# Expert feed-forward: the first two token tiles of an expert as a pair with the weights stationary

## Chip, cores and metric

One core of a Trainium2 chip runs the whole program. The time is device microseconds (us) of one execution; the kernel before has a median of 1525.64 us over three runs (1524.73 to 1525.66).

## What is computed

A transformer layer on 2 x 1024 tokens of width 512. After a layer norm, the output is the sum of the input, causal attention (16 heads, 4 key groups), a shared two-layer network, and a mixture of 32 experts of which each token uses 6. Cut to the part that the change touches:

```python
idx, w = _route(xf, Wr, br)                    # 6 experts for each of 2048 tokens
gate = zeros((T, E)).at[arange(T)[:, None], idx].add(w)
def step(acc, ew):
    w1, w2, g = ew                             # w1 256 x 512, w2 512 x 256
    h = square(relu(xf @ w1.T)) @ w2.T
    return acc + g[:, None] * h, None
```

Only the chosen tokens are computed. The six choices of 2048 tokens are 12288 rows, which the router sorts by expert into tiles of 128 rows, each expert's last one filled up.

## The kernel before, in words

There are three stages. The first normalises and routes the tokens and computes the shared network. The second, which the change rebuilds, runs the experts. The third runs the attention of eight groups and adds the experts' rows, fetched by index.

Every product of 32-bit values is made of three matmuls on reduced-width values: an upper half (`_hi`) and a lower half (`_lo`, what the upper half leaves out), as upper x upper, upper x lower and lower x upper. ScalarE makes each upper half by a copy, VectorE each lower half by a subtraction.

The program of the expert stage is written out by hand, one in-order list for each engine, and every hand-over is a semaphore count. `over_experts` loops over 8 rounds of 4 experts; inside, a body per expert takes its tiles `lo` to `hi`, which `count_tiles` has worked out from the routing (at least 2 tiles each). A tile's steps are:

- GpSimd gathers 128 token rows into one of four slots of `xg`.
- TensorE turns them (`transpose_gathered`, four 128-column matmuls into `ps_x`), a tile ahead of their use; ScalarE copies the upper half (`upper_tokens`), VectorE the lower (`lower_tokens`).
- `hidden_tile`: 12 matmuls of 256 columns, tokens stationary, first-layer weights moving.
- ScalarE takes relu (`relu_hidden`), VectorE squares (`square_hidden`), TensorE turns the squares (`transpose_hidden`, two 128-column matmuls), ScalarE and VectorE make halves again (`upper_hidden`, `lower_hidden`).
- `output_tile`: 6 matmuls of 512 columns; ScalarE copies the result to `ysb` (`copy_output`), SyncE stores it to memory.

TensorE's list is one tile deep: first layer of tile p and the turn of tile p+1's tokens, second layer of tile p-1, turn of tile p's squares. So the second layer of an expert's last tile stands inside the next expert's body.

The weights of an expert are 1 MB of raw values. SyncE loads them into one of two buffers `eraw`, three experts ahead; ScalarE and VectorE convert them in four pieces (`upper_weights`, `lower_weights`) into one of four slots, two experts ahead. SyncE's list is in order too, and is what `store_tiles` says:

```python
sp.wait_ge(ew_lo, (e + (NSH + 2)) * WP)
sp.dma_start(eraw[:, (s + AHEAD) % 2, :], we[bass.ds((e + AHEAD) * P, P), :])
...
with sp.Fori(lo, hi) as p:
    ...
    sp.wait_ge(y_copied, past(p + 1))
    sp.dma_start(y_d[bass.ds(p * P, P), :], ysb[:, ...])
```

The load for expert e+3 thus stands behind the store of the last tile of expert e-1, which waits for that tile's output copy. The change leaves SyncE's and GpSimd's lists as they are.

In the first stage the router marks, for every token tile, which of at most `MAXT` = 160 tiles its rows go to (`mark_rows` on VectorE, rows `tile_hot` of `MAXT` columns), and the memory of the tiles that might stay unused is filled with zeros by one DMA from ScalarE's queue.

Of the kernel before, what the change touches and what calls it, by code (L numbers as in the profile page):

```python
# [6 lines left out]
F32 = mybir.dt.float32  # L7
# [38 lines left out]
MAXT = MINT + 2 * E  # L46
XG = 4
YB = 4
# [80 lines left out]
def moe_attention_kernel(nc, x, wa, we, wr, br, out):  # L129
# [11 lines left out]
    with ExitStack() as ctx:  # L141
# [75 lines left out]
        with ExitStack() as room:  # L217

            xg = sb("xg", [P, XG, D], F32, room)
            xgT_hi = sb("xgT_hi", [P, KD, P], F32R, room)  # L220
            xgT_lo = sb("xgT_lo", [P, KD, P], F32R, room)
# [3 lines left out]
            hT_hi = sb("hT_hi", [P, KM, P], F32R, room)  # L225
            hT_lo = sb("hT_lo", [P, KM, P], F32R, room)
# [38 lines left out]
        ps_y = ps_s[:, 3, :]  # L265

# [391 lines left out]
        def _(pe):  # L658
# [190 lines left out]
            def transpose_gathered(slot, q):  # L849
                pe.wait_ge(xg_in[slot], (q // XG + 1) * 16)  # L850
                for k in range(KD):
                    mm = pe.transpose(ps_x[:, k * P:(k + 1) * P], xg[:, slot, k * P:(k + 1) * P], ident[:, :])
                mm.then_inc(mx_ready, 1)

            def hidden_tile(p, s):
# [3 lines left out]
                for k in range(KD):  # L859
                    pe.matmul(ps_h, xgT_hi[:, k, :], w_hi[:, k, :], start=(k == 0), stop=False)  # L860
                    pe.matmul(ps_h, xgT_hi[:, k, :], w_lo[:, k, :], start=False, stop=False)  # L861
                pe.wait_ge(mx_lo, p + 1)
                for k in range(KD):
                    mm = pe.matmul(ps_h, xgT_lo[:, k, :], w_hi[:, k, :], start=False, stop=(k == KD - 1))  # L864
                mm.then_inc(mh_ready, 1)
                q = p + 1
                with pe.If(q // 2 % 2 == 0):
                    with pe.If(q % 2 == 0):
                        transpose_gathered(0, q)
                    with pe.Else():  # L870
                        transpose_gathered(1, q)
                with pe.Else():
                    with pe.If(q % 2 == 0):
                        transpose_gathered(2, q)
                    with pe.Else():
                        transpose_gathered(3, q)

            def output_tile(p, s):

                w_hi, w_lo = w2(hi_slot(s)), w2(lo_slot(s))  # L880
                pe.wait_ge(mhhi_ready, past(p + 1))
                for m in range(KM):
                    pe.matmul(ps_y, hT_hi[:, m, :], w_hi[:, m, :], start=(m == 0), stop=False)  # L883
                    pe.matmul(ps_y, hT_hi[:, m, :], w_lo[:, m, :], start=False, stop=False)  # L884
                pe.wait_ge(mhlo_ready, past(p + 1))
                for m in range(KM):
                    mm = pe.matmul(ps_y, hT_lo[:, m, :], w_hi[:, m, :], start=False, stop=(m == KM - 1))  # L887
                mm.then_inc(my_ready, 1)

            def transpose_hidden(p, weights=None):  # L890
                pe.wait_ge(mhsq_ready, past(p + 1))
                for m in range(KM):
                    if m and weights is not None:

                        pe.wait_ge(ew_lo, weights)
# [9 lines left out]
            def expert_tiles(e, s, lo, hi, es):  # L905

                pe.wait_ge(ew_lo, (e + NSH) * WP + 2)
                hidden_tile(lo, slot_of(s))
                after = pair_bound(pe, e + 2)
                if s:  # L910
                    output_tile(lo - 1, slot_of(s - 1))
                else:
                    with pe.If(es > 0):
                        output_tile(lo - 1, slot_of(SLOTS - 1))
# [9 lines left out]
            output_tile(last - 1, slot_of(SLOTS - 1))  # L924
# [95 lines left out]
        def _(act):  # L1020
# [206 lines left out]
            def upper_tokens(q):  # L1227

                act.wait_ge(mx_ready, q + (1 + XG))
                act.activation(xgT_hi[:, :, :], ps_x.rearrange("p (k n) -> p k n", k=KD), ACT.Copy).then_inc(mx_hi, 1)  # L1230
# [12 lines left out]
            def upper_hidden(p):  # L1243
# [570 lines left out]
```

## Time and profile before

| what | value |
|---|---|
| median of three runs | 1525.64 us |
| profiled execution | 1526.73 us, span 1525.0 us |
| TensorE busy | 1509.9 us (99% of the span) |
| VectorE / ScalarE / GpSimd busy | 1132.8 / 837.9 / 298.3 us |
| moved by DMA | 184.34 MB, mean 121 GB/s |
| chain that ended last | 96% TensorE, 2% VectorE, 1% DMA |
| granted TensorE clock | 0.999 of full |

The span is the profiled execution from its first to its last instruction; 1.7 us lie around it. An engine's busy time says how full it is, not whether it decides. "Idle before" and its releaser say what an instruction waited for. A time that has a row of its own is a start, in us from the start of the span. Two instructions that start 0.12 us apart and last 0.28 us overlap in the engine's pipeline: the distance of the starts is what one costs in a row.

### The profile page before, as it was taken

The page shows a single profiled execution, that of the slowest core. Times are in us where ns is not written, and L with a number is a line of the kernel's source. Part 1 is how long each engine was busy: PE and PEld are TensorE (multiplying, and loading weights), DVE is VectorE, ACT ScalarE, POOL GpSimd, SP SyncE. Part 2 cuts the span into 40 slices and gives each one's busy share as a digit, 9 for nine tenths or more (in the row PEclk, how much of TensorE's full clock was granted, in tenths as well). Part 3 has the DMA queues.
Part 4 walks back from the last instruction along what each step waited for, and adds up shares of the span by engine and source line. Part 5 has one row for each costly group of instructions (what it writes and reads, how often), then busy time and mean ns, then how long its engine had stood idle before and what let it go on. Part 6 is the DMA issues. An engine that isn't in the chain of part 4 may idle for free.

```text
span 1525.0 us, 31150 instructions
## 1 busy us (share of the span) xinstructions
PE 1509.9 (99%) x8552; PEld 1302.1 (85%) x8553; DVE 1132.8 (74%) x2586; ACT 837.9 (55%) x1753; POOL 298.3 (20%) x540
## 2 busy tenths in 40 slices
PE   9998999999999999999999999999999999999998
PEld 8877998899899888888888888888888888888886
DVE  7896666666666669859949948967975994994896
ACT  5574666666666635535625635644553553553553
POOL 0003344334344311011002002102102101200211
PEclk9999999999999999999999999999999999999999
DMA  8874777777876612102102103422211210210111
GB/s 318 301 302 165 218 243 233 229 234 228 258 234 207 228 35 70 43 21 76 55 7 79 45 28 120 149 62 85 67 34 41 69 41 21 76 34 28 56 42 55
DMA packets 64774, 184.34 MB, mean 121 GB/s; under 512 B 7136, under 2 KB 7264, under 8 KB 60000
## 3 DMA queue, kind: packets, MB, share of 16 engines
q1 hardware_dynamic: 39888, 112.56, 21.1%
q0 software_dynamic: 16640, 54.54, 13.1%
q10 hardware_dynamic: 8208, 16.78, 2.8%
q8 instruction: 19, 0.31, 0.1%
q14 instruction: 19, 0.16, 0.0%
HBM read 123.29 MB, written 60.56 MB: 121 GB/s over the span
## 4 chain that ended last, share of the span: by engine, by line
PE 96%; DVE 2%; DMA 1%; issue 0%; ACT 0%; ACTq 0%; DVEq 0%; SPq 0%
PE bank L663 8%; PE bank L665 8%; PE bank L993 8%; PE bank L664 8%; PE ps_s L663 7%; PE ps_s L665 7%; PE ps_s L664 7%; PE ps_s L980 5%; PE ps_s L982 5%; PE ps_s L981 4%; PE ps_s L860 4%; PE ps_s L883 4%; PE ps_s L864 3%; PE ps_s L861 3%; PE ps_s L887 3%; PE ps_s L884 3%
## 5 line engine op out<-in xcount | busy, mean ns | idle before, releaser
L1322 ACT ACTIVATE probs<-probs,negmax 128x128 f32<-128x128 f32 (+7 forms) x256 | 197.4, 774 | 122.5 <-DVE negmax L1736 121.9
L1330 ACT ACTIVATE pT_hi<-bank 128x512 fp32r<-128x512 f32 x288 | 164.5, 595 | 143.4 <-PE bank L993 117.5
L1347 DVE TENSOR_TENSOR pT_lo<-bank,pT_hi 128x512 fp32r<-128x512 f32 x288 | 189.7, 684 | 41.0 <-ACT pT_hi L1330 40.0
L1736 DVE CUSTOM_DVE_ANT_0 probs<-ps_s,causal 128x128 f32<-128x128 f32 (+7 forms) x256 | 189.5, 753 | 17.1 <-PE ps_s L982 14.9
L427 POOL TENSOR_TENSOR settled<-ident 128x1 f32<-128x1 f32 x192 | 46.5, 242 | 788.7 <-DVE acc L1765 778.7
L993 PE MATMUL bank<-ident,probs 128*128 128x128 f32 x1152 | 157.0, 272 | 0.0
L993 PEld LDWEIGHTS bank<-ident,probs 128*128 128x128 f32 x1152 | 136.9, 141 | 19.8
L663 PE MATMUL ps_s<-xT_hi,wa_hi 128*128 128x512 f32 x384 | 152.7, 398 | 0.0
L665 PE MATMUL ps_s<-xT_hi,wa_lo 128*128 128x512 f32 x384 | 150.9, 393 | 0.0
L664 PE MATMUL ps_s<-xT_lo,wa_hi 128*128 128x512 f32 x384 | 150.2, 391 | 0.0
L1745 DVE TENSOR_SCALAR probs<-probs,rnorm 128x128 f32<-128x128 f32 (+7 forms) x256 | 133.4, 521 | 9.1
L980 PE MATMUL ps_s<-kT_hi,qT_hi 128*128 128x512 f32 (+5 forms) x384 | 134.0, 349 | 1.0 <-DVE qT_lo L1716 0.5
L982 PE MATMUL ps_s<-kT_hi,qT_lo 128*128 128x512 f32 (+5 forms) x384 | 131.2, 342 | 0.0
L981 PE MATMUL ps_s<-kT_lo,qT_hi 128*128 128x512 f32 (+5 forms) x384 | 130.9, 341 | 0.0
L663 PE MATMUL bank<-pT_hi,v_hi 128*128 128x512 f32 x288 | 123.6, 429 | 0.6 <-DVE cT_lo L1347 0.6
L623 POOL DMA_INDIRECT xg<-normed_tokens,comb_idx x112 | 111.8, 998 | 23.3 <-issue 18.1
L1347 DVE TENSOR_TENSOR hT_lo<-ps_s,hT_hi 128x256 fp32r<-128x256 f32 x111 | 47.2, 425 | 92.0 <-ACT hT_hi L1245 53.5
L665 PE MATMUL bank<-pT_hi,v_lo 128*128 128x512 f32 x288 | 113.5, 394 | 0.0
L1251 ACT ACTIVATE ysb<-ps_s 128x512 f32 x111 | 66.5, 599 | 84.9 <-PE ps_s L887 65.7
L664 PE MATMUL bank<-pT_lo,v_hi 128*128 128x512 f32 x288 | 112.7, 391 | 0.0
L652 POOL DMA_INDIRECT comb<-expert_outputs,comb_idx x96 | 105.2, 1096 | 19.6 <-issue 11.5
L663 PE MATMUL bank<-wa_hi,cT_hi 128*128 128x512 f32 x256 | 101.5, 396 | 1.4 <-DVE cT_lo L1347 1.4
(197 smaller groups left out, 3596.3 us busy)
## 6 DMA issues: line engine op xcount, KB each, us to landing
eraw<-we SPq DMA_DIRECT2D x37, 1024.0 KB
expert_outputs<-ysb SPq DMA_DIRECT2D x111, 256.0 KB
araw<-wa SPq DMA_DIRECT2D x37, 512.0 KB, 4.3
expert_outputs<-comb ACTq DMA_DIRECT2D x1, 16384.0 KB, 47.4
normed_tokens<-xn SPq DMA_DIRECT2D x4, 1024.0 KB, 10.0
out<-acc SPq DMA_DIRECT2D x16, 256.0 KB
acc<-x SPq DMA_DIRECT2D x2, 1024.0 KB, 13.8
turned_tokens<-xT_hi SPq DMA_DIRECT2D x2, 1024.0 KB, 7.6
```

Of the source, the lines that this page charges most:

```text
L663: pe.matmul(out_, lh, rh, start=(first and k == 0), stop=False)
L664: pe.matmul(out_, lh, rl, start=False, stop=False)
L665: mm = pe.matmul(out_, ll, rh, start=False, stop=(last and k == parts - 1))
L980: pe.matmul(o, q_h, kT_hi[:, ks], start=True, stop=False)
L981: pe.matmul(o, q_h, kT_lo[:, ks], start=False, stop=False)
L982: mm = pe.matmul(o, q_l, kT_hi[:, ks], start=False, stop=True)
L993: mm = pe.transpose(ps_t[blk % 2][:, h * P:(h + 1) * P], probs[:, i % 2, h, a * P:(a + 1) * P], ident[:, :])
L1322: act.activation(pr, pr, ACT.Exp, bias=negmax[:, i % 2, a:a + 1], scale=-1.0, accum_out=rowsum[:, i % 2, a:a + 1]).then_inc(exp_ready, 1)
L1330: act.activation(pT_hi[:, blk % RING, :], ps_t[blk % 2][:, :], ACT.Copy).then_inc(pt_hi_ready, 1)
L1347: dve.tensor_tensor(out_, whole, upper.bitcast(F32), ALU.subtract).then_inc(signal, 1)
L1736: dve.tensor_tensor_reduce(halves(probs[:, i % 2, a, 0:keys]), ps_s[:, s:s + parts, 0:keys // parts], halves(causal[:, SQ - keys:]), -1.0, ...
L1745: dve.tensor_scalar(pr, pr, rnorm[:, i % 2, a:a + 1], None, ALU.mult).then_inc(probs_ready, 1)
```

## The change

An expert has at least three tiles now (`LEAST`), and its first two are taken as a pair. `hidden_pair` runs the first layer with the weights stationary and the tokens of both tiles moving (256 columns), once for each half of the hidden units, so its result stands with hidden units on partitions and need not be turned. ScalarE takes its relu and its square, which is at once the upper half; VectorE squares and subtracts. The second tile's tokens are turned at the head of the body into a bank of their own (`ps_x2`). The second layer of the expert before's last tile is split: its upper half's matmuls stand ahead of the pair's first layer, its lower half's behind it and behind the third tile's turn. The second layer of the pair's first tile follows in the body (`output_first`), that of the second in the loop. In the loop, the turn of the squares stands between the upper and the lower half of the second layer. `hT_hi` and `hT_lo` have two sets and a place for either tile. The list of tiles grows from 160 to 177 columns, and so do the marks and the zero fill. The attention's first maximum on VectorE waits for the expert stage's stores, since its buffer shares memory with the new ones.

```diff
-MAXT = MINT + 2 * E
+LEAST = 3
+MAXT = max(LEAST * (E - n) + min(n * TILES, (T * TOPK + (P - 1) * n) // P) for n in range(E + 1))
...
+            def hidden_pair(lo, s):
...
+                both = lambda x, k: x[:, k, :, :].rearrange("p t n -> p (t n)")
+                for m in range(KM):
+                    ms = slice(m * P, (m + 1) * P)
+                    if m == 0:
+                        pe.wait_ge(mx_hi, lo + 2)
+                    for k in range(KD):
+                        pe.matmul(ps_p[m], w_hi[:, k, ms], both(xgT_hi, k), start=(k == 0), stop=False)
+                        pe.matmul(ps_p[m], w_lo[:, k, ms], both(xgT_hi, k), start=False, stop=False)
+                    if m == 0:
+                        pe.wait_ge(mx_lo, lo + 2)
+                    for k in range(KD):
+                        mm = pe.matmul(ps_p[m], w_hi[:, k, ms], both(xgT_lo, k), start=False, stop=(k == KD - 1))
+                    mm.then_inc(mh_ready, 1)
...
             def expert_tiles(e, s, lo, hi, es):
 
-                pe.wait_ge(ew_lo, (e + NSH) * WP + 2)
-                hidden_tile(lo, slot_of(s))
-                after = pair_bound(pe, e + 2)
+                turn_tokens(lo + 1, ps_x2)
                 if s:
-                    output_tile(lo - 1, slot_of(s - 1))
+                    output_upper(lo - 1, s - 1, ps_y2)
...
-                transpose_hidden(lo, (e + (NSH + 1)) * WP)
-                with pe.Fori(lo + 1, hi) as p:
+                after = pair_bound(pe, e + 2)
+                pe.wait_ge(ew_lo, (e + NSH) * WP + 2)
+                hidden_pair(lo, slot_of(s))
+                pe.sem_inc(mt_ready, 2)
+                turn_tokens(lo + 2, ps_x)
+                if s:
+                    output_lower(lo - 1, s - 1, ps_y2)
...
+                pe.wait_ge(ew_lo, (e + (NSH + 1)) * WP)
+                output_first(lo, s)
+                with pe.Fori(lo + 2, hi) as p:
                     hidden_tile(p, slot_of(s))
-                    output_tile(p - 1, slot_of(s))
+                    pe.wait_ge(y_copied, past(p - 1))
+                    output_upper(p - 1, s, ps_y)
                     transpose_hidden(p)
+                    output_lower(p - 1, s, ps_y)
                 return after
...
             def expert_uppers(e, s, lo, hi, es):
...
-                relu_hidden(lo)
-                upper_tokens(lo + 1)
-                upper_weights(0, slot, arrived)
                 if s:
-                    copy_output(lo - 1)
+                    upper_tokens(lo + 1, 1)
...
-                upper_hidden(lo)
+                upper_weights(0, slot, arrived)
                 after = pair_bound(act, e + 2)
                 upper_weights(1, slot, arrived)
-                with act.Fori(lo + 1, hi) as p:
+                relu_pair(lo, 0)
+                upper_pair(lo, 0, s)
+                upper_weights(2, slot, arrived)
+                relu_pair(lo, 1)
+                upper_pair(lo, 1, s)
+                upper_tokens(lo + 2)
+                if s:
+                    copy_output(lo - 1, ps_y2)
...
+                copy_output(lo, ps_y)
+                upper_weights(3, slot, arrived)
+                with act.Fori(lo + 2, hi) as p:
                     relu_hidden(p)
                     upper_tokens(p + 1)
-                    copy_output(p - 1)
-                    upper_hidden(p)
-                upper_weights(2, slot, arrived)
-                upper_weights(3, slot, arrived)
+                    upper_hidden(p, s)
+                    copy_output(p - 1, ps_y)
```

VectorE's list follows ScalarE's in the same order. How the lists of the built programs read, first ScalarE in the body of the second expert, before. `mrelu` is the relu, `xgT_hi` the turned tokens, `w_hi` a piece of weights (it needs the raw load), `ysb` the output copy, `hT_hi` the hidden upper half:

```order
L1241 ACTIVATE mrelu<-ps_s 128x256
L1229 REGISTER_ALU
L1230 ACTIVATE xgT_hi<-ps_s 128x512
L1234 ISA
L1235 ACTIVATE w_hi<-eraw 128x512
L1251 ISA
L1251 ACTIVATE ysb<-ps_s 128x512
```

The output copy is the fourth piece of work in the body. The same place of the changed kernel, from the head of the body (`prelu` is the pair's relu):

```order
L1280 ACTIVATE xgT_hi<-bank 128x4x128
...
L1286 ACTIVATE w_hi<-eraw 128x512
...
L1298 ACTIVATE prelu<-bank 128x256
...
L1303 ACTIVATE hT_hi<-prelu 128x256
L1286 ACTIVATE w_hi<-eraw 128x512
L1298 ACTIVATE prelu<-bank 128x256
...
L1303 ACTIVATE hT_hi<-prelu 128x256
...
L1280 ACTIVATE xgT_hi<-ps_s 128x4x128
L1314 ISA
L1314 ACTIVATE ysb<-bank 128x512
```

The output copy of the expert before (`ysb<-bank`) now stands behind both relus and squares of the pair, the third tile's tokens and three pieces of weights (the second of them is in a gap here), and the first piece stands ahead of the relus. TensorE's loop body, for the tiles that are not in the pair, before:

```order
L852 MATMUL ps_s<-ident,xg 128x128 x4
...
L883 MATMUL ps_s<-wa_hi,hT_hi 128x512
L884 MATMUL ps_s<-wa_lo,hT_hi 128x512
L883 MATMUL ps_s<-wa_hi,hT_hi 128x512
L884 MATMUL ps_s<-wa_lo,hT_hi 128x512
L887 MATMUL ps_s<-wa_hi,hT_lo 128x512 x2
L891 REGISTER_ALU
L896 MATMUL ps_s<-ident,mhsq 128x128 x2
```

and now:

```order
L858 MATMUL ps_s<-ident,xg 128x128 x4
...
L920 MATMUL ps_s<-wa_hi,hT_hi 128x512
L921 MATMUL ps_s<-wa_lo,hT_hi 128x512
L920 MATMUL ps_s<-wa_hi,hT_hi 128x512
L921 MATMUL ps_s<-wa_lo,hT_hi 128x512
L932 REGISTER_ALU
L934 MATMUL ps_s<-ident,mhsq 128x128 x2
L928 MATMUL ps_s<-wa_hi,hT_lo 128x512 x2
```

The turn of the squares has moved ahead of the last two matmuls of the second layer.

## Rows read from the trace of the kernel before

**Rows 1.** Busy time of each engine in two stretches, with header: expert stage, first gap.

```profile
core 0: us, PE busy (x) PEld busy (x) DVE busy (x) ACT busy (x) POOL busy (x), PEclk, DMA share, GB/s
138.00:140.00 2.00, 0.00 (x0) 0.00 (x0) 2.00 (x5) 0.45 (x1) 1.38 (x3) 1.00 0.69 254
135.80:534.10 398.30, 393.70 (x2665) 352.61 (x2664) 246.84 (x467) 265.19 (x572) 158.24 (x323) 1.00 0.73 233
```

**Rows 2.** Costliest groups of 140 to 540 us, by shape: turns of squares.

```profile
L896 PE MATMUL ps_s<-ident,mhsq 128*128 128x128 f32 x222 | 42.8, 274 | 2.6 <-DVE mhsq L1653 2.3 <-issue 0.3
```

**Rows 3.** Timeline of TensorE, one tile of the stage (start, duration, instruction).

```profile
163.05 0.38 PE L896 MATMUL ps_s<-ident,mhsq 128*128 128x128 f32 x2
...
163.39 0.28 PE L861 MATMUL ps_s<-wa_lo,xgT_hi 128*128 128x256 f32 x1
...
164.22 0.65 PE L864 MATMUL ps_s<-wa_hi,xgT_lo 128*128 128x256 f32 x4
164.70 0.60 PE L852 MATMUL ps_s<-ident,xg 128*128 128x128 f32 x4
165.06 0.47 PE L883 MATMUL ps_s<-wa_hi,hT_hi 128*128 128x512 f32 x1
165.37 0.39 PE L884 MATMUL ps_s<-wa_lo,hT_hi 128*128 128x512 f32 x1
...
166.06 0.62 PE L887 MATMUL ps_s<-wa_hi,hT_lo 128*128 128x512 f32 x2
166.52 0.38 PE L896 MATMUL ps_s<-ident,mhsq 128*128 128x128 f32 x2
```

**Rows 4.** Timeline of TensorE, ScalarE, VectorE: start of one expert, its output copy, conversions.

```profile
205.69 0.36 PE L860 MATMUL ps_s<-wa_hi,xgT_hi 128*128 128x256 f32 x1
...
209.38 0.60 ACT L1251 ACTIVATE ysb<-ps_s 128x512 f32 x1 [0.30 <-PE ps_s L887]
...
214.33 0.60 PE L852 MATMUL ps_s<-ident,xg 128*128 128x128 f32 x4
214.53 0.38 ACT L1241 ACTIVATE mrelu<-ps_s 128x256 f32<-128x256 f32 x1 [0.64 <-PE ps_s L864]
...
214.95 0.42 DVE L1653 TENSOR_TENSOR mhsq<-mrelu 128x256 f32<-128x256 f32 x1 [0.60 <-ACT mrelu L1241]
...
218.29 0.39 ACT L1241 ACTIVATE mrelu<-ps_s 128x256 f32<-128x256 f32 x1
...
218.56 0.61 ACT L1230 ACTIVATE xgT_hi<-ps_s 128x512 fp32r<-128x512 f32 x1
...
219.04 0.65 ACT L1235 ACTIVATE wa_hi<-eraw 128x512 fp32r<-128x512 f32 x1
```

**Rows 5.** Timeline of SyncE's queue: weight loads, output stores between them.

```profile
211.29 0.35 SPq L490 DMA_DIRECT2D eraw<-we  x1
214.04 7.27 SPq L500 DMA_DIRECT2D expert_outputs<-ysb  x3
221.77 0.35 SPq L490 DMA_DIRECT2D eraw<-we  x1
```

**Rows 6.** Timelines of SyncE's queue and ScalarE: weight loads and conversions that waited.

```profile
137.37 0.33 SPq L472 DMA_DIRECT2D eraw<-we  x1
...
142.19 0.63 ACT L1235 ACTIVATE w_hi<-eraw 128x512 fp32r<-128x512 f32 x1 [3.73 <-DMA eraw<-we]
...
247.33 0.35 SPq L490 DMA_DIRECT2D eraw<-we  x1
...
255.37 0.63 ACT L1235 ACTIVATE w_hi<-eraw 128x512 fp32r<-128x512 f32 x1 [0.78 <-DMA eraw<-we]
...
356.36 0.35 SPq L490 DMA_DIRECT2D eraw<-we  x1
...
364.65 0.63 ACT L1235 ACTIVATE wa_hi<-eraw 128x512 fp32r<-128x512 f32 x1 [0.22 <-DMA eraw<-we]
```

**Rows 7.** Busy time of each engine in two stretches after the load of 221.77.

```profile
222.50:228.00 5.50, 5.50 (x40) 4.97 (x39) 2.47 (x5) 2.92 (x7) 2.66 (x6) 1.00 0.90 355
228.00:228.50 0.50, 0.50 (x6) 0.50 (x6) 0.42 (x1) 0.00 (x0) 0.00 (x0) 1.00 0.08 33
```

**Rows 8.** DMA issues of the page, timelines of ScalarE's queue and VectorE: fill, marks.

```profile
expert_outputs<-comb ACTq DMA_DIRECT2D x1, 16384.0 KB, 47.4
...
55.37 0.44 ACTq L1183 DMA_DIRECT2D expert_outputs<-comb  x1
...
112.69 2.87 DVE L1526 TENSOR_SCALAR tile_hot<-lane,xf,tok_f 128x160 f16<-128x160 f16 x12
```

More of the change, by code:

```diff
@@ L265, in moe_attention_kernel @@
         ps_y = ps_s[:, 3, :]
+        ps_x2 = banks[0][:, :]
+        ps_p = [bank[:, 0:2 * P] for bank in banks[1::2]]
+        ps_y2 = banks[2][:, :]
         consts_in = sem("consts_in")
@@ new lines, in output_first @@
+            def output_first(lo, s):
+                w_hi, w_lo = w2(hi_slot(slot_of(s))), w2(lo_slot(slot_of(s)))
+                for m in range(KM):
+                    pe.wait_ge(mhhi_ready, past(lo + (m + 1)))
+                    pe.matmul(ps_y, hT_hi[:, s % 2, m, 0, :], w_hi[:, m, :], start=(m == 0), stop=False)
+                    pe.matmul(ps_y, hT_hi[:, s % 2, m, 0, :], w_lo[:, m, :], start=False, stop=False)
+                    pe.wait_ge(mhlo_ready, past(lo + (m + 1)))
+                    mm = pe.matmul(ps_y, hT_lo[:, s % 2, m, 0, :], w_hi[:, m, :], start=False, stop=(m == KM - 1))
+                mm.then_inc(my_ready, 1)
@@ L885, in output_tile, with output_lower, transpose_hidden @@
+            def output_lower(p, s, bank):
+                w_hi = w2(hi_slot(slot_of(s)))
                 pe.wait_ge(mhlo_ready, past(p + 1))
                 for m in range(KM):
-                    mm = pe.matmul(ps_y, hT_lo[:, m, :], w_hi[:, m, :], start=False, stop=(m == KM - 1))
+                    mm = pe.matmul(bank, hT_lo[:, s % 2, m, 1, :], w_hi[:, m, :], start=False, stop=(m == KM - 1))
                 mm.then_inc(my_ready, 1)
-            def transpose_hidden(p, weights=None):
+            def transpose_hidden(p):
@@ L1259, in _ @@
             upper_tokens(0)
+            upper_tokens(1, 1)
             for c in range(WP):
@@ L1682, in expert_lowers @@
                 slot = slot_of(s + 2)
[L1683 to L1684 removed]
+                if s:
+                    lower_tokens(lo + 1, 1)
+                else:
+                    with dve.If(es > 0):
+                        lower_tokens(lo + 1, 1)
                 lower_weights(e + 2, 0, slot)
[L1686 removed]
                 after = pair_bound(dve, e + 2)
                 lower_weights(e + 2, 1, slot)
[L1689 removed]
+                square_pair(lo, 0)
+                lower_pair(lo, 0, s)
+                lower_weights(e + 2, 2, slot)
+                square_pair(lo, 1)
+                lower_pair(lo, 1, s)
+                lower_tokens(lo + 2)
+                lower_weights(e + 2, 3, slot)
+                with dve.Fori(lo + 2, hi) as p:
                     square_hidden(p)
                     lower_tokens(p + 1)
[L1692 to L1694 removed]
+                    lower_hidden(p, s)
                 return after
```

121 lines of the change are left out of this document (73 added, 48 removed).

## Prediction

> **What bounds the kernel now.** I read the busy times of the stage first, then TensorE's timeline, then the queue that feeds the weights. In the expert stage (135.80 to 534.10 us) TensorE is busy 393.70 of 398.30 us, while ScalarE and VectorE have a third of the stage free and the DMA engines work at 0.73 of their time [rows 1]. So TensorE sets the end, and whatever leaves its list comes back as time, as long as nothing else becomes late. The stage has 111 tiles: 222 turns of squares, two a tile [rows 2]. One undisturbed tile lasts 163.05 to 166.52, 3.47 us [rows 3]. It is 12 first-layer matmuls of 256 columns at 0.119 us (seven steps from 163.39 to 164.22), 6 second-layer matmuls of 512 columns at 0.23 us (three steps from 165.37 to 166.06), and six 128-column turns, four of tokens and two of squares, which share the rest: 3.47 - 1.43 - 1.40 = 0.64, or 0.11 us each. All matmuls ran at the full one of TensorE's two clocks, granted share 1.00 [rows 1].
>
> **The change, part by part.** *Turns of squares.* The pair's first layer has the weights stationary and 256 columns of tokens moving, so the 24 matmuls of two tiles keep their count and width (24 x 0.119), and the result stands turned already. Each of 32 experts drops four turns: 32 x 4 x 0.11 = **-14.1 us**. The last tile's second layer is only cut in two, with the same six matmuls; in the loop it is cut round the turn of squares. That turn now comes 0.44 + 0.93 us after the first layer instead of 0.44 + 1.40. Its squares need relu (0.20 after the first layer, 0.38 long [rows 4]), a VectorE square (0.42 [rows 4]) and two hand-overs, some 1.1 us; it fits, with 0.2 to spare, so I price it at nothing. Without that cover it would cost tenths for each of 47 single tiles.
>
> *The minimum of three tiles.* It would add whole tiles where an expert had two. SyncE's rows show how many tiles each expert stores between two weight loads: 3, 4 or 5 [rows 5]. Counted over all its loads, 20 experts have three, 9 four, 3 five, together the 111. None has two, so no tile is added.
>
> *A short wait at the head of each body.* The pair waits for the second tile's upper half, copied from its turn. Behind the turn stand 0.93 us of second layer; the copy comes after the copy of an output (slot 0.5), takes 0.61 [rows 4], and starts some 0.85 after the body. It ends 0.15 late: 31 x 0.15 = **+4.7 us**.
>
> *The router in front.* The tile count grows from 160 to 177 columns. VectorE's 96 rows of tile marks take 0.23 us for 160 columns (2.87 us for 12) [rows 8], and it is nearly always busy there; bounds 0 (hidden) and 96 x 17/160 x 0.23 = 2.3; I take **+1.5 us**, nearer the upper end as TensorE waits for the last marks. The zero fill grows by 17 x 256 KB; at the 16384 KB in 47.4 us of [rows 8] that is up to 13 us more. Issued at 55.37 it lands by 116 instead of 103, and the load that SyncE holds behind it went out at 137.37 [rows 6], so nothing. VectorE's new wait ahead of the first maximum lies behind eight projections of twelve 512-column matmuls, 22 us, against some 6 us for the last stores: nothing.
>
> *The moved output copy, the term that decides.* SyncE works in order: it issues the load of expert e+3's raw weights (1 MB) only after it has stored the last tile of expert e-1. Before, that tile's copy on ScalarE starts one tile into body e (209.38, in a body that began at 205.69 [rows 4]), and the load goes out 1.9 us later, at 211.29 [rows 5]. The first conversion that needs these raw weights comes at 219.04 [rows 4], so a load of three-tile bodies has 7.75 us. Now the last tile's lower half waits until the whole pair is through. With T the start of a body on TensorE: turn 0.44, upper half 0.93, wait 0.15, pair 2.85 = T+4.37; relu, square and the copy of the next tokens stand before the output copy, which starts at T+5.8; load at T+7.7. A body of three tiles lasts 0.44 + 0.93 + 0.15 + 2.85 + 0.44 + 0.47 + 1.40 + 3.48 = 10.16, and the next body's first conversion now comes early, 1.35 after its start, ahead of the pair's relu. The load has 10.16 + 1.35 - 7.7 = **3.8 us** instead of 7.75. If it lands at W after the body's start instead, everything behind it on ScalarE slides: two conversions, relu, square, a conversion, relu, square and the token copy put the output copy at W+3.5 and the next load at W+5.35; squares and lower halves reach TensorE so that the pair's second layer ends at W+4.55, and one more tile ends the body at W+8.0. So after a three-tile body the next W is 5.35 + L - 8.0 = L - 2.65, with L from issue to landing, and a three-tile body lasts L + 5.35, against 10.16 without the wait. The stretch is L - 4.8 for each of the 19 bodies that follow one of three tiles. After four or five tiles the load has 3.5 us more and costs nothing below L = 8.
>
> L is what the trace shows least, as a load that lands in time has no row. Four landings were waited for. The first, on nearly idle engines, took 142.19 - 137.37 = 4.8 us, the lower end; later ones took 255.37 - 247.33 = 8.0 and 364.65 - 356.36 = 8.3 [rows 6], the upper end. In between stand bounds: the load of 221.77 had landed when the engines fell idle at 228.0 (355 GB/s until then, 33 after) [rows 7], so L was at most 6.2. The new order places two output stores close round each load and a gather at its end, much like the case of rows 7, so I take L = 6.3: 19 x 1.5 = **+28.5 us**. Its ends: 0 at 4.8, 19 x 3.4 = +65 at 8.2.
>
> The sum is -14.1 + 4.7 + 1.5 + 28.5 = +20.6. The profiled execution took 1526.73 us (span 1525.0), 1.1 above the median of 1525.64, so 1547.3 for a profiled one and **1546 us** for the median. Zero is at 19 x (L - 4.8) = 7.9, L = 5.2.
>
> A rule of the notes speaks for the other side. The Trainium skill, in "DMA: Bandwidth & Descriptors", section "Anatomy of one DMA", fits a transfer as about 2.0 us fixed plus bytes over 436 GB/s. By that estimate 1 MB lands in 4.4 us, the weight term is zero and the sum is -7.9. The first load of the trace, 4.8 us, agrees nearly; the 8.0 and 8.3 us landings do not.
>
> **The rivals.**
> - *The loads are quick (L below 5.2).* Their time is then hidden and the dropped turns are worth something: -14.1 + 4.7 + 1.5 = -7.9, 1518 us, faster. For it speaks the 4.8 us landing and that a waiting kernel issues less other traffic; against it that stores and gathers of 256 KB run beside every later load, at 0.73 of the engines' time. Chance 0.17.
> - *The loads are as slow as the two late waits.* L = 8 gives 19 x 3.2 = 61 and +53, 1579 us. For it: stores of two outputs are now issued back to back with the load. Against: it would have shown as a wait in the old kernel at most three-tile bodies, where 7.4 to 8 us were to be had, and four waits are all there were. Chance 0.13.
> - *The clock falls in the new gaps.* The old kernel has one gap of over 2 us, with the granted clock still 1.00 (138 to 140, nothing busy) [rows 1]; the new gaps are 0.5 to 1 us each, two or three in a body. If the clock fell to the lower level of 1.2 GHz for some 3 us in each of 19 bodies, that costs up to 19 x 1.5 = 28 on top, 1574 us. The Trainium skill, "TensorE: Matmul & The Clock Gate", names idle TensorE time as what throttles it. Chance 0.03.
> - *No difference*, L within 0.15 of 5.2: 1526. Chance 0.05.
>
> **How the numbers follow.** The forecast branch (L from 5.4 to 7.3, 1530 to 1565) has 0.62. The faster rival gives 0.17 for faster by over 0.2% (3 us, about what a measurement can tell here), the fourth gives 0.05, the rest 0.78 is slower. The range runs from 1518, the quick loads, to 1577, just short of the slow ones.
>
> **What would show it.** If right: many ScalarE conversions (first piece of an expert) wait for the raw weight load, near 19 times and 1 to 3 us each, where four did; TensorE's waits before the pair's second layer name ScalarE's or VectorE's halves; load issues come 7.5 to 9 us after a body starts; three-tile bodies last near 11.6 us, four-tile bodies after a longer one 13.6. Turns of squares fall from 222 to 94. If the conversions do not wait on the load, the prediction is wrong in its main term; if they wait but bodies last under 11 us, L was too large. If the stage is longer and no load is waited for, something that I priced at nothing (the squares in the loop, the head of the body) has taken over.

## The result, and the profile after

| | kernel before | kernel after |
|---|---|---|
| median | 1525.18 us (1523.57 to 1525.66, 4 runs) | 1554.24 us (1551.57 to 1557.4, 4 runs) |
| profiled execution | 1526.73 us, span 1525.0 us | 1551.57 us, span 1549.8 us |
| expert stage, first turn to end of last second layer | 135.80 to 534.32 us: 398.5 | 135.16 to 561.89 us: 426.7 |
| from there to the end of the span | 990.7 us | 987.9 us |

The ratio is 1.0193, 95% interval 1.0171 to 1.0215: the change makes the kernel slower. The forecast was 1546 us, range 1518 to 1577, with 0.78 on slower. The profiled execution after is the fastest of its four runs, so the spans differ by 24.8 us where the medians differ by 29.1; the accounts below are made between the spans.

The page of the kernel after, parts 1, 4 and 6: busy times, what the chain that ended last is made of, and DMA issues with the median time from issue to landing.

```profile
PE 1510.6 (97%) x8424; PEld 1282.5 (83%) x8425; DVE 1136.0 (73%) x2586; ACT 850.7 (55%) x1753; POOL 304.3 (20%) x540
...
PE 74%; DMA 8%; issue 8%; DVE 4%; ACT 2%; SPq 1%; POOL 1%; ACTq 1%; DVEq 0%; POOLq 0%
DMA eraw<-we 7%; PE bank L669 7%; PE bank L1043 7%; PE bank L671 7%; PE bank L670 7%; PE ps_s L669 6%; PE ps_s L671 6%; PE ps_s L670 6%; PE ps_s L1030 4%; PE ps_s L1032 4%; PE ps_s L1031 4%; DVE tile_hot L1598 1%; PE ps_s L858 1%; PE ps_s L908 1%; PE ps_s L907 1%
...
eraw<-we SPq DMA_DIRECT2D x37, 1024.0 KB, 6.6
expert_outputs<-comb ACTq DMA_DIRECT2D x1, 20736.0 KB, 61.7
```

TensorE's share of the span falls to 97%, and in the chain that ended last the raw weight loads now have 7%. That share counts a load from its issue to its landing, so it is more than what the engines waited. The page of the kernel before gave no landing for them; now the median of all 37 is 6.6 us. Four of these stand ahead of the stage; the 33 of the stage have 4.8 to 8.4 us and a median of 6.3. The fill grew from 16384 KB in 47.4 us [rows 8] to 20736 KB in 61.7, and nothing waited for it.

The stage and two stretches of its first body, busy time by engine (columns as in [rows 1]); the first row answers to the stage's row there:

```profile
135.16:561.89 426.73, 399.15 (x2538) 334.66 (x2536) 251.44 (x468) 280.46 (x575) 164.93 (x323) 0.99 0.66 217
...
139.00:143.00 4.00, 1.01 (x9) 0.77 (x8) 1.34 (x3) 1.37 (x3) 1.36 (x3) 1.00 1.00 411
143.00:148.00 5.00, 4.00 (x13) 2.84 (x14) 3.42 (x7) 3.07 (x8) 0.00 (x0) 0.66 0.86 355
```

The same work in TensorE's list less 128 turns takes 28.4 us more than the 398.30 of [rows 1] (28.2 by the table, which counts the last matmul of the stage to its end); the DMA share falls from 0.73 to 0.66, so the stage does not move more, it waits more. The turns of squares, from the costliest groups of 130 to 570 us by shape, are 94 where [rows 2] has 222:

```profile
L934 PE MATMUL ps_s<-ident,mhsq 128*128 128x128 f32 x94 | 18.0, 273 | 0.1
```

The waits of the stage, grouped by who waits for whom (total us, times, longest):

```profile
ACT wa_hi L1286 <- DMA eraw<-we: 25.6, 11, 2.9
...
PEld bank L858 <- issue: 18.0, 31, 1.1
ACT w_hi L1286 <- DMA eraw<-we: 16.9, 10, 3.5
...
PEld bank L883 <- ACT xgT_hi L1280: 14.1, 32, 1.0
PE ps_s L899 <- DVE hT_lo L1419: 10.8, 28, 0.7
...
PE ps_s L896 <- ACT hT_hi L1303: 7.2, 7, 3.7
```

ScalarE waits 21 times for a raw weight load, 25.6 + 16.9 = 42.5 us in all. The two PEld rows are TensorE's weight loading at the head of a body: the first turn, for which the trace names nobody, and the pair's first layer. The last two rows are TensorE in the pair's second layer, at work that ScalarE and VectorE finish late.

One three-tile body and the start of the next, from the timelines of TensorE, ScalarE and SyncE's queue; these rows answer to [rows 4] and [rows 5]:

```profile
236.48 0.65 PE L858 MATMUL bank<-ident,xg 128*128 128x128 f32 x4
...
237.79 1.28 ACT L1286 ACTIVATE wa_hi<-eraw 128x512 fp32r<-128x512 f32 x2
...
242.21 0.59 ACT L1314 ACTIVATE ysb<-bank 128x512 f32 x1
...
243.90 0.35 SPq L496 DMA_DIRECT2D eraw<-we  x1
...
247.23 0.65 PE L858 MATMUL bank<-ident,xg 128*128 128x128 f32 x4 [0.51 <-issue]
...
247.92 0.60 ACT L1280 ACTIVATE xgT_hi<-bank 128x512 fp32r<-128x512 f32 x1 [0.42 <-PE bank L858]
...
250.15 1.29 ACT L1286 ACTIVATE w_hi<-eraw 128x512 fp32r<-128x512 f32 x2 [1.63 <-DMA eraw<-we]
...
253.79 0.59 ACT L1314 ACTIVATE ysb<-bank 128x512 f32 x1
...
254.74 0.50 PE L899 MATMUL ps_s<-wa_hi,hT_lo 128*128 128x512 f32 x1 [0.51 <-DVE hT_lo L1419]
```

The body begins with the turn at 236.48 (T). The two conversions at 237.79 come ahead of the pair's relu. The last tile's output copy starts at 242.21, T+5.7, and the load goes out only at 243.90, T+7.4. The conversion that needs it would be free to start about 1.35 after the next body's start at 247.23, and starts at 250.15, 6.25 after the issue, with 1.63 us of waiting put down to the load. Everything behind it on ScalarE slides: relu, square, the output copies (253.79), and TensorE waits at 254.74 for the lower half of the square. Then the next load is late too.

### The profile page after: what moved, and what is told of

It reads as the page before. It is cut to its first block, busy times and chain, and to the rows that moved or that the text cites. A ratio compares the mean times of both kernels' runs of the same rounds, so it can differ in the third digit from the quotient of the medians.

```text
span 1549.8 us, 30938 instructions
## 1 busy us (share of the span) xinstructions
PE 1510.6 (97%) x8424; PEld 1282.5 (83%) x8425; DVE 1136.0 (73%) x2586; ACT 850.7 (55%) x1753; POOL 304.3 (20%) x540
## 4 chain that ended last, share of the span: by engine, by line
PE 74%; DMA 8%; issue 8%; DVE 4%; ACT 2%; SPq 1%; POOL 1%; ACTq 1%; DVEq 0%; POOLq 0%
DMA eraw<-we 7%; PE bank L669 7%; PE bank L1043 7%; PE bank L671 7%; PE bank L670 7%; PE ps_s L669 6%; PE ps_s L671 6%; PE ps_s L670 6%; PE ps_s L1030 4%; PE ps_s L1032 4%; PE ps_s L1031 4%; DVE tile_hot L1598 1%; PE ps_s L858 1%; PE ps_s L908 1%; PE ps_s L907 1%
## 5 line engine op out<-in xcount | busy, mean ns | idle before, releaser
L629 POOL DMA_INDIRECT xg<-normed_tokens,comb_idx x112 | 117.1, 1045 | 24.1 <-issue 18.8
L671 PE MATMUL bank<-wa_hi,cT_lo 128*128 128x512 f32 x256 | 100.0, 391 | 0.0
L670 PE MATMUL bank<-wa_lo,cT_hi 128*128 128x512 f32 x256 | 99.7, 390 | 0.0
## 6 DMA issues: line engine op xcount, KB each, us to landing
expert_outputs<-comb ACTq DMA_DIRECT2D x1, 20736.0 KB, 61.7
```

The lines of the kernel that those rows point to most:

```text
L670: pe.matmul(out_, lh, rl, start=False, stop=False)
L671: mm = pe.matmul(out_, ll, rh, start=False, stop=(last and k == parts - 1))
```

## The experiments

All times are medians; ratios are against the kernel before, run on the same chip in the same batch, with 95% intervals. "Body" is the distance between the turns at the heads of two experts.

| run | what it is | us | before | ratio |
|---|---|---|---|---|
| e1_early_load | after, raw weights loaded earlier | 1520.29 | 1524.08 | 0.9973 [0.9963, 0.9983] |
| e2_before_late_load | before, raw weights loaded later | 1557.20 | 1524.08 | 1.0217 [1.0200, 1.0234] |
| e4_late_pieces | after, conversions later | 1555.07 | 1524.08 | 1.0199 [1.0182, 1.0216] |
| e7_early_copy | after, output copy earlier | 1548.72 | 1524.08 | 1.0170 [1.0149, 1.0191] |
| e5b_split_undone | e1, second layer in one piece | 1526.54 | 1525.33 | 1.0007 [0.9997, 1.0017] |
| e6b_turn_behind | e1, turn of squares last | 1522.16 | 1525.33 | 0.9984 [0.9975, 0.9993] |
| e8b_first_body | e1, first body's conversions later | 1517.22 | 1525.33 | 0.9946 [0.9933, 0.9960] |
| e10_tail_behind_loop | e8b, a half step behind the loop | 1519.12 | 1525.43 | 0.9961 [0.9947, 0.9975] |
| f4_four_waits | before, four idle waits on TensorE | 1524.04 | 1525.43 | 0.9994 [0.9984, 1.0003] |
| f9_nine_waits | before, nine idle waits on TensorE | 1523.95 | 1525.43 | 0.9999 [0.9989, 1.0009] |

### Is the late load the cause? Cure it, and make it without the rest

**e1_early_load.** The changed kernel; SyncE issues the next raw load right behind the store of a body's first tile, not behind its last. The raw buffers are just free by then.

```
+load_raw(0)                  # ahead of all bodies
 def store_tiles(e, s, lo, hi, es):
-    load_raw(e)              # raw weights of expert e + 3
     after = pair_bound(sp, e + 2)
-    with sp.Fori(lo, hi) as p: (store tile p)
+    store_from(lo, lo + 1)
+    load_raw(e + 1)          # raw weights of expert e + 4
+    store_from(lo + 1, hi)
```

> The changed kernel, but SyncE issues the raw weights of expert e+4 right behind the store of body e's first tile (before: those of e+3 behind the store of the expert before's last tile). ScalarE, VectorE and TensorE keep their lists. Late load theory: each load has some 10 us instead of 3.8, the 21 waits for raw weights (42.5 us on ScalarE) fall to none or one or two, three-tile bodies that follow one of three tiles fall from 11.9 to about 10.5 us (what those after a longer body last now), and the time falls to 1517 to 1523 us. Rival, the pair's body itself is slow (waits for lower halves, the head of the body) and the waits for weights only stand in its shadow: the waits go, but the time stays above 1540.

Measured: 1520.29 us, 0.9973 [0.9963, 0.9983], as the load theory expects. ScalarE waits for a load once, 3.0 us in the first body; of the waits of TensorE and its weight loading these are the longest left:

```profile
PEld bank L875 <- issue: 17.6, 31, 1.1
...
PEld bank L900 <- ACT xgT_hi L1297: 8.8, 32, 0.9
...
PEld ps_s L913 <- DVE w_lo L1436: 3.8, 1, 3.8
PE ps_s L913 <- ACT hT_hi L1320: 3.6, 1, 3.6
```

The stage takes 529.79 - 134.55 = 395.2 us against 426.7. In one body (T = 230.87) the load goes out at 240.75 and is used two bodies later, not in the next. Bodies of three tiles behind one of three last 10.47 us on average, against 11.95 in the kernel after.

**e2_before_late_load.** The kernel before, untouched on its compute engines, with the same number of loads but each behind the store of a body's first tile.

```
 def store_tiles(e, s, lo, hi, es):
-    (load the raw weights of expert e + 3)
-    after = pair_bound(sp, e + 2)
-    with sp.Fori(lo, hi) as p: (store tile p)
+    store_from(lo, lo + 1)
+    (load the raw weights of expert e + 3)
+    after = pair_bound(sp, e + 2)
+    store_from(lo + 1, hi)
```

> The kernel before with one edit on SyncE: the load of e+3 goes out behind the store of body e's first tile, one tile (3.5 us) later than it did, so about 4.2 us are left between load and use in a three-tile body. Late load theory: the old kernel slows as the changed one did, since a landing takes some 6.6 us: 19 bodies x (6.6 - 4.2 - about 0.9 of slack) = +28, 1545 to 1565 us, with some 20 waits for raw weights on ScalarE. Rival, the old order of ScalarE's list (relu and tokens ahead of the first piece) hides a late load: under 1532.

Measured: 1557.20 us, 1.0217 [1.0200, 1.0234]. Its waits and its row of DMA issues:

```profile
ACT wa_hi L1242 <- DMA eraw<-we: 21.1, 9, 4.1
...
ACT w_hi L1242 <- DMA eraw<-we: 18.6, 7, 3.7
PE ps_s L890 <- ACT hT_hi L1252: 17.9, 12, 2.7
...
eraw<-we SPq DMA_DIRECT2D x37, 1024.0 KB, 6.8
```

The late load alone, without pair, split or any other part of the change, makes the same kind of waits (39.7 us in 16) and about the same loss. With e1 this is both halves of the proof: the place of the load is enough to lose the time, and moving it forward is enough to regain it.

A part of this loss is the clock. Three single waits of TensorE, 1.9 to 2.7 us, for upper halves that ScalarE makes behind its own wait for a load were each followed by a stretch at a lower granted clock: 0.66 in 226 to 231, 0.57 in 278 to 286 and 0.57 in 387 to 391. A fourth stands in the first body, behind a wait of 2.3 us for the squares that the late load did not cause (columns as in [rows 1]):

```profile
138.00:142.00 4.00, 3.50 (x19) 3.48 (x19) 1.79 (x5) 1.41 (x3) 1.16 (x2) 0.57 1.00 417
```

The granted clock of e2's stage is 0.98 in the mean, where the stages of e1 and of the kernel after have 0.99. If TensorE had always had work, two hundredths of 431 us would be some 9 us; this estimate is an upper bound, and the rest of the loss is waiting.

### Two cures that only moved the wait

**e4_late_pieces.** The changed kernel with the load as late as it is, but its conversions behind the output copies (two) and behind the loop (two), on ScalarE; on VectorE the lower parts likewise.

```
-upper_weights(0, ...)   # head of the body; 1 and 2 follow round the first relu
-upper_weights(1, ...)
-upper_weights(2, ...)
 copy_output(lo, ps_y)
-upper_weights(3, ...)
+upper_weights(0, ...)
+upper_weights(1, ...)
 with act.Fori(lo + 2, hi) as p: ...
+upper_weights(2, ...)
+upper_weights(3, ...)
```

> The changed kernel with SyncE's list as it is, but ScalarE and VectorE convert the pieces of the weights late in the body: two behind the output copies, two behind the loop. The load still goes out late, its use comes 6 us later. Late load theory: waits for raw weights gone, 1517 to 1527 us (the pieces may delay a relu in the loop by tenths). Rival: stays above 1540.

Measured: 1555.07 us, a miss by nearly 30, in the range that the rival gave. The cure works on its target: no row names the load any more. But the waits of e4 have new heads:

```profile
PEld bank L883 <- ACT xgT_hi L1280: 31.9, 32, 1.4
...
PEld ps_s L934 <- DVE mhsq L1738: 21.5, 32, 1.5
...
PE bank L883 <- ACT xgT_hi L1280: 18.0, 30, 0.9
```

And the head of one body, from the timelines of TensorE and ScalarE:

```profile
271.05 0.65 PE L858 MATMUL bank<-ident,xg 128*128 128x128 f32 x4
...
271.17 0.60 ACT L1314 ACTIVATE ysb<-ps_s 128x512 f32 x1 [0.23 <-PE ps_s L928]
...
271.66 1.14 ACT L1286 ACTIVATE w_hi<-eraw 128x512 fp32r<-128x512 f32 x2
...
272.70 0.59 ACT L1280 ACTIVATE xgT_hi<-bank 128x512 fp32r<-128x512 f32 x1
...
273.34 0.39 PE L883 MATMUL bank<-xgT_hi,w_hi 128*128 128x256 f32 x1 [0.72 <-ACT xgT_hi L1280]
```

The turn of tokens is issued at 271.05, but ScalarE has an output copy and two weight conversions ahead of the copy of these tokens, which starts at 272.70 instead of some 0.65 behind the turn, and the pair begins at 273.34, 2.3 after the turn. Every body pays this, not only those behind a three-tile one: three-tile bodies last 11.83 us on average, four-tile bodies 15.05. I had counted the conversions as free at the end of a body because ScalarE has a third of the stage free; the free third is not at the end of a body.

**e7_early_copy.** The changed kernel with the last tile's second layer in one piece ahead of the pair and its output copy right behind the token copy, so that the load goes out early with SyncE as it is.

```
 # TensorE
 output_upper(lo - 1, ...)
+output_lower(lo - 1, ...)
 hidden_pair(lo, ...)
 turn_tokens(lo + 2, ps_x)
-output_lower(lo - 1, ...)
 # ScalarE
 upper_tokens(lo + 1, 1)
+copy_output(lo - 1, ps_y2)
 upper_weights(0, ...)
 ...
-copy_output(lo - 1, ps_y2)
```

> The changed kernel with the last tile's second layer in one piece ahead of the pair, and its output copy right behind the second tile's tokens on ScalarE; SyncE's list is untouched, so the load goes out about 3.5 us earlier, as in the old kernel. Late load theory: 7.4 us between load and use against a landing of 6.6: few waits, each under 1 us, 1517 to 1530 us. Rival (the split or the pair is the cost, not the copy's place): above 1540.

Measured: 1548.72 us, again a miss, and again in the rival's range; but e1 keeps the pair and the split and is fast, so they are not the cost by themselves. The only wait for the load left is that of the first body, but:

```profile
PEld ps_s L899 <- DVE hT_lo L1413: 43.5, 64, 1.1
...
ACT ysb L1311 <- PE bank L928: 24.2, 26, 1.3
...
PE ps_s L899 <- DVE hT_lo L1413: 15.7, 31, 0.6
```

ScalarE now stands still for TensorE's bank (24.2 us), ahead of both the conversions and the pair's relu. So the lower halves of the pair's squares are late for TensorE (15.7 us in 31 waits) and three-tile bodies last 11.46 us, behind short and long bodies alike.

### What the parts of the change are worth with the load in time

**e5b_split_undone.** e1 with TensorE's list as in the diff of e7: the last tile's second layer in one piece ahead of the pair. ScalarE stays as in e1.

> The early-load kernel with the last tile's second layer in one piece again ahead of the pair. Theory 'the split earns its place': one body loses 0.47 us of cover behind the pair, so TensorE waits at the first tile's lower halves for VectorE, about 0.5 us in each of 31 bodies as in the early-copy run, and saves only its 8.8 us of waits for the token copy at the head; near 1527 (1522 to 1535), against 1520.3. Rival, the split buys nothing once the load is early: the head waits go and no new ones come, 1511 to 1518.

Measured: 1526.54 us; e1 was 1520.29 beside a kernel before of 1524.08. The split is worth 5 us or so. The 8.8 us at the head of the pair fell to 0.9, and behind the pair came new ones:

```profile
PEld ps_s L916 <- DVE hT_lo L1433: 12.8, 33, 0.5
...
PEld ps_s L913 <- ACT hT_hi L1317: 7.0, 31, 0.2
...
PEld bank L900 <- ACT xgT_hi L1294: 0.9, 1, 0.9
```

**e6b_turn_behind.** e1 with the turn of the squares behind both halves of the second layer in the loop.

```
 output_upper(p - 1, s, ps_y)
-transpose_hidden(p)
 output_lower(p - 1, s, ps_y)
+transpose_hidden(p)
```

> The early-load kernel with the turn of the squares behind both halves of the second layer in the loop again. Theory of the prediction: the turn between the halves is free, and putting it back gains at most the 1.2 us of waits seen at the turn; but the copy of the turned squares then comes 0.47 us later, against 0.35 us of token turn at the head of the next body, so up to 0.3 us in each of 31 bodies: 1519 to 1530, near 1525. Rival, the turn inside costs time that the waits do not show: below 1517.

Measured: 1522.16 us, ratio 0.9984 [0.9975, 0.9993] against e1's 0.9973 [0.9963, 0.9983]. The intervals overlap, so no difference is shown: by the two medians the turn inside costs nothing and is worth at most a microsecond or two. The larger of the two costs that I expected, up to 0.3 us a body, is not there.

**e8b_first_body.** The first body is a case of its own. Its load is the one of 137.37 in [rows 6], waited for by both kernels. e8b is e1 with the four conversions of that body alone moved as in e4.

```
+with act.If(es == 0):    # first body: behind the output copies, behind the loop
+    upper_weights(0, ...); upper_weights(1, ...)
 with act.Fori(lo + 2, hi) as p: ...
+with act.If(es == 0):
+    upper_weights(2, ...); upper_weights(3, ...)
```

> The early-load kernel with the raw-weight conversions of the first body alone put behind its output copies (two pieces) and behind its loop (two). Theory: TensorE's 3.6 us wait at the first body's second layer and the lower granted clock that follows it are worth some 5 us together; 1514 to 1517, with the first body near 14 us instead of 19.5. Rival 1: the clock falls anyway and only part of the wait goes: 1517 to 1519. Rival 2: the late pieces hold the loop and the next body, no gain: 1520 to 1523.

Measured: 1517.22 us, the fastest version here, 0.9946 [0.9933, 0.9960] against the kernel before. By the two ratios that is 0.0027 or 4.1 us below e1, short of the 5 that the theory gave. The time lies 0.2 us outside the theory's range and inside that of the first rival, but that rival's reason, that the clock falls anyway, did not come true. The same two stretches of the first body (columns as in [rows 1]), in e1:

```profile
139.00:143.00 4.00, 0.41 (x4) 0.18 (x3) 1.34 (x3) 2.06 (x5) 1.36 (x3) 0.80 1.00 415
143.00:148.00 5.00, 4.97 (x16) 3.75 (x17) 3.21 (x8) 2.69 (x6) 0.00 (x0) 0.50 0.72 294
```

in e8b:

```profile
139.00:143.00 4.00, 2.57 (x19) 2.13 (x18) 2.63 (x6) 2.27 (x6) 1.22 (x3) 1.00 0.89 372
143.00:148.00 5.00, 4.79 (x30) 3.79 (x30) 3.28 (x7) 2.78 (x6) 1.47 (x4) 1.00 1.02 412
```

and in the kernel before:

```profile
143.00:148.00 5.00, 4.52 (x26) 3.60 (x27) 3.24 (x7) 3.09 (x8) 1.53 (x3) 1.00 1.01 405
```

In e1 TensorE waits for 3.6 us. Its granted clock is 0.80 in the mean of 139 to 143 and 0.50, which is 1.2 GHz, over the whole of 143 to 148, and the same matmuls of 256 columns stand 0.21 us apart instead of 0.12. Sixteen matmul records fit where e8b has thirty. In e8b and in the kernel before the clock stays at 1.00. The first body goes from 19.55 to 15.56 us, not to the 14 that I expected; wait and lower clock together are the 4 us. The late pieces also hold the second body, 18.21 us instead of 17.37, as the second rival had it, so the stage of the profiled execution gains 3.2 us.

**e10_tail_behind_loop.** e8b with TensorE's loop turned by half a step, so that the last lower half stands behind the loop's exit; the order of the matmuls is the same.

```
-with pe.Fori(lo + 2, hi) as p:
-    hidden_tile(p); output_upper(p - 1); transpose_hidden(p); output_lower(p - 1)
+tile(lo + 2)             # hidden_tile, output_upper, transpose_hidden
+with pe.If(hi > lo + 3):
+    with pe.Fori(lo + 3, hi) as p:
+        output_lower(p - 2); tile(p)
+output_lower(hi - 2)
```

> The first-body kernel with TensorE's loop turned by half a step: the lower half of the last tile but one stands behind the loop's exit, the order of the matmuls stays. Theory: the 31 gaps at the head of a body, 17.6 us in all for which the trace names no releaser, are TensorE's sequencer on its way out of the loop and through the branches of the next turn; with 0.47 us of matmuls to issue in between they shrink to 0.1 or so, and 3-tile bodies go from 10.5 to 10.1: 1505 to 1512. Rival: the gaps belong to the branches of the turn alone, or the new branch round the loop costs as much: 1515 to 1519.

Measured: 1519.12 us, 0.9961 [0.9947, 0.9975]: no gain on e8b. By the medians a microsecond or two is lost, but the intervals overlap. The gap ahead of the head's turn is still there:

```profile
PEld bank L875 <- issue: 18.3, 31, 1.1
...
PEld bank L900 <- ACT xgT_hi L1304: 10.0, 32, 1.2
```

So the loop's exit is not what makes it. It may be the two nested branches by which the turn picks one of four token buffers: in the loop the same branches lie behind twelve matmuls and show no gap. The Trainium skill, in "Advanced Engine Details and Errata", section "Control Flow Timing", gives some 108 ns for a compare-and-branch and 51 for a plain one, which by that estimate is 0.2 to 0.3 us for two and a jump. No run here separates them; this stays open.

### The 2.8 us outside the stage

Every version of the changed kernel ends 987.7 to 988.0 us after its stage; of the versions of the kernel before, the one compared here ends 990.7 us after it, and e2 and the two runs below 990.2 to 990.3. The code of the attention groups is the same, and one group takes 122.35 us instead of 122.67 (between ScalarE's first copies of keys of one group and the next); the difference builds up in small steps over the group.

**f4_four_waits** and **f9_nine_waits.** The kernel before with idle waits on TensorE between stage and attention.

```
 output_tile(last - 1, slot_of(SLOTS - 1))
+for _ in range(4):       # f9: 9
+    pe.wait_ge(started, 4)
```

> The kernel before, with four waits on TensorE that are long fulfilled put between the last tile of the experts and the attention groups. All changed kernels run each attention group in 122.35 us, the kernel before and its late-load version in 122.67, with the same code. Theory: that is where TensorE's instructions happen to lie, and four more (or nine, next run) move them: a group of 122.35 us in at least one of the two, 1522.5 in all. Rival, it has another cause (buffers that moved): 122.67 in both, 1525.3.

> As the run with four waits, with nine. Same theories: 122.35 us a group in at least one of the two, or 122.67 in both.

Measured: 1524.04 and 1523.95 us, both within their interval of no change, and a group takes 122.67 us in both. Where the instructions happen to lie, at least by shifts of this size, is not the cause. It stays open.

## Why the prediction was right, and where its terms were off

The direction and the mechanism held; every sign that was to show it right was there except in the front. How near the number came is partly luck, as the first two points show. By the spans:

- *The late load, forecast +28.5.* The stage of the kernel after less that of e1 is 426.7 - 395.2 = **31.5 us**. Forecast were near 19 waits of 1 to 3 us, measured 21 of 2.0 on average. In the 11 three-tile bodies behind one of three tiles the stretch is 11.95 - 10.47 = 1.48 us, as forecast (1.5); it is larger in the longer bodies that follow one of three tiles, 2.1 us in each of five with four tiles (15.90 against 13.83) and 2.6 in each of two with five. A three-tile body was to last L + 5.35; with the stage's median L of 6.3 that is 11.65, and the gap at the head of the body, measured below, is the other 0.3. The load went out at T+7.4 in the body shown, forecast T+7.7. Four-tile bodies behind a longer one lasted 13.92, forecast 13.6.
- *L, taken as 6.3.* The number came true in the new order, but the row that it was read from says something else. [rows 7] was taken to show that the load of 221.77 had landed when the DMA engines fell to a share of 0.08 at 228.0. In f9, which is the kernel before up to the end of the stage, the same load goes out at 221.76, the DMA share falls in the same way, and the load lands 7.4 us after its issue, at 229.2:

```profile
eraw<-we SPq DMA_DIRECT2D x1, 1024.0 KB, 7.4
...
228.00:228.50 0.50, 0.50 (x6) 0.50 (x6) 0.42 (x1) 0.00 (x0) 0.00 (x0) 1.00 0.08 33
```

A low mean over 16 engines does not say that the last one is done. The loads of the old order have medians of 7.5 (f4) and 7.3 us (f9). With L = 7.4 the forecast's own sum would have been 19 x 2.6 - 7.9 = +41.5, not +20.6. That the new order's loads would be quicker than the old one's, 6.3 against 7.4, was not foreseen; here the number was lucky.
- *The dropped turns, forecast -14.1, and the short wait at the head, +4.7.* Together -9.4, or -0.30 a body. In e1, where nothing else is late, the other 31 bodies give 395.2 - 398.5 - (19.55 - 16.84) = **-6.0 us**, -0.19 a body (16.84 are the first four tiles of the kernel before). The wait for the token copy was not too small: the 8.8 us at L900 are idle time of weight loading, most of it beside running matmuls. By the starts of the matmuls in e1 the pair begins late by 1.3 us in all 31 bodies. What I priced at nothing is the gap ahead of the body's first turn, which stands behind a loop's exit and branches. From e1's timeline:

```profile
261.82 0.71 PE L945 MATMUL ps_s<-wa_hi,hT_lo 128*128 128x512 f32 x2
262.52 0.65 PE L875 MATMUL bank<-ident,xg 128*128 128x128 f32 x4
```

Two matmuls of 512 columns at 0.23 us would let the turn begin at 262.28; it begins 0.24 later. Over the 31 heads this gap is 0.31 us on average, **9.5 us** together, and the trace names nobody for it. With -14.1 and +1.3 that makes -3.3; the other -2.7 of the measured -6.0 are not accounted for.
- *The router, forecast +1.5.* Not to be read from the two profiles: the stage begins at 135.16 instead of 135.80, but the kernel before had a stretch of lower clock in its first stage (granted 0.83 in 50 to 60) which the kernel after had not (1.00). Among executions at a granted 1.00 ahead of the stage, it begins at 134.08 (f4) and 134.21 (e2) with the old router, and at 134.50 (e7), 134.55 (e1) and 135.16 (after) with the new one. The marks' 17 columns more thus cost 0.3 to 1.1 us, between the bounds and below what I took; the -0.6 of the spans goes with the clock.
- *What I priced at nothing.* The fill, the wider minimum, the squares turned in the loop: right, e6b shows the last. The first body: wrong. It lasts 19.2 us against 16.84, since its conversions now stand ahead of the relu and wait for the load of [rows 6], and the granted clock of 143 to 148 us is 0.66. That is the clock rival, which had 0.03, in two bodies of 32 and not in 19. The other one is the body that starts at 374.40, and there no single wait was over 0.7 us; TensorE was busy 3.61 of 5 us before:

```profile
378.00:383.00 5.00, 3.61 (x21) 2.31 (x19) 3.62 (x8) 4.13 (x9) 2.06 (x3) 1.00 0.40 153
383.00:387.00 4.00, 4.00 (x19) 3.96 (x20) 1.60 (x3) 1.61 (x4) 0.00 (x0) 0.57 0.86 265
```

By these rows the two cost at most 0.34 x 5 + 0.43 x 4 = 3.4 us. The first body of e1 alone costs about as much (0.20 x 4 + 0.50 x 5 = 3.3), so the 31.5 us of the late load hold next to nothing of the clock.
- *Outside the stage,* -2.8 us that no term foresaw and no run explained.

The sum by spans: 31.5 - 6.0 + 2.7 - 0.6 - 2.8 = 24.8 us; forecast 20.6. In the medians, 1554.2 against 1546.

Beside the rival of quick loads the prediction put the fit of the Trainium skill, "DMA: Bandwidth & Descriptors". Its section, in full "Anatomy of one DMA — SWDGE (gpsimd) path", gives the fit for transfers that GpSimd issues; these loads are SyncE's, so the 4.4 us for 1 MB was an estimate carried over from another path. The loads issued just ahead of the stage or at its start took 4.7 to 4.9 us in the runs that show them, near it. No median of a run agrees: 5.6 in e1, 6.6 after, 6.8 in e2 and e7, where loads run beside the gathers and the stores.

The two misses of e4 and e7 say where my picture was too simple. I took ScalarE as a list with room in it. It has room over the stage, but at the head of a body, the copy of the tokens, and behind the pair, relu and square, have none, and whatever is put there is paid in every body.

## What to carry to other kernels

When a producer's copy is moved later, follow the in-order queue that waits for it: here a store held a weight load behind it, and its price, about 31 us, was several times what the dropped work gave. Moving the load ahead of the stores kept the change and turned 1.9% slower into 0.3% faster, and with the first body mended into 0.5%. An engine's free share says nothing of the place where a moved instruction is put; look at what waits behind it in each body. A load that lands in time has no wait, and the one profile of the kernel before gave no landing either; the profiles of f4 and f9, whose stage is the same, give one for every load. So measure the landing in a second profile before you price a window with it. The loads that were waited for (8.0 and 8.3 us) would have been too long a guess, and the end of a busy stretch of DMA (6.2) was too short a one.

## What the runs showed of the hardware

- The time of one 1 MB load from issue to landing is not one number: the page's medians over all 37 are 5.6 us in e1, 6.6 after, 6.8 in e2 and e7. It is 7.5 in f4 and 7.3 in f9, which in their stage are the kernel before, and there only three loads each were waited for. So the old order had loads slower than the 6.3 I assumed and hid them; that the new order slowed the load itself is not what happened.
- A load can still be on its way when the DMA engines look idle: in f9 the mean share is 0.08 in 228.0 to 228.5, and the load of 221.76 lands at 229.2.
- The granted clock fell behind waits of TensorE of 3.6 us (first body of e1, then 0.50 over 5 us), of 1.9 to 2.7 us (four times in e2, then 0.57 to 0.66), and once in the kernel after without a wait over 0.7 us, behind a stretch in which TensorE was busy 3.61 of 5.00 us. The kernel before idles 2.0 us at the place of [rows 1], in a wait of 2.3 us, and kept 1.00, while e2 behind a wait of the same 2.3 us had 0.57. So no length of wait that decides can be read from these runs. The Trainium skill, "TensorE: Matmul & The Clock Gate", section "Part 1: The HAM clock gate", names idle TensorE time as the cause; the waits of e1 and e2 agree.
